# Edge passes of a graph network: gather in halves, bf16 scatter, packed control words, stored one-hots

## Time and profile before

| | |
|---|---|
| median of 3 runs | 13450.17 us (13437.72 to 13457.99) |
| span of the profiled execution | 13453.0 us |
| the three message layers | from about 1688 to 4347 us |
| relation pass | 4689 to 5909 us |
| two SAGE passes | 5946 to 7141 us |
| attention and the end | from about 7150 us |
| busy: TensorE, VectorE, ScalarE, GpSimd | 83%, 81%, 39%, 18% |

### The profile page before, as it was taken

One profiled execution on the slowest core, in us unless ns is written; L12 is line 12 of the kernel. 1 busy time (PEld: TensorE's weight loads), 2 busy tenths in 40 slices (PEclk: granted clock), 3 DMA queues, 4 the chain that ended last, 5 costly groups with the idle time before them and its releaser, 6 DMA issues. The chain is left out here.

```text
span 13453.0 us, 456368 instructions
## 1 busy us (share of the span) xinstructions
PE 11137.4 (83%) x106911; PEld 9882.7 (73%) x106912; DVE 10911.2 (81%) x40164; ACT 5227.5 (39%) x19100; POOL 2409.1 (18%) x7659
## 2 busy tenths in 40 slices
PE   3555399899899599976665879999998789999998
PEld 3444388799798499975553339999997338999998
DVE  6545399688688288876565999999997999999998
ACT  1000022122222022235452338865453337875454
POOL 2777300000000000001110001112221001222222
PEclk9999999899899599999896999999998999999999
DMA  1111177444243011113231554432221554432222
GB/s 54 47 50 47 45 228 236 138 128 128 80 128 115 4 41 41 41 50 88 71 87 51 148 140 115 115 92 73 70 73 47 143 147 113 115 98 73 70 73 61
DMA packets 1206840, 1232.94 MB, mean 92 GB/s; under 512 B 218352, under 2 KB 1042801, under 8 KB 1206107
## 3 DMA queue, kind: packets, MB, share of 16 engines
q1 hardware_dynamic: 1180954, 1228.47, 32.8%
q0 software_dynamic: 25792, 3.35, 0.2%
HBM read 1115.06 MB, written 116.16 MB: 92 GB/s over the span
## 5 line engine op out<-in xcount | busy, mean ns | idle before, releaser
L993 DVE TENSOR_SCALAR hot<-iota_row,place 128x128 f32<-128x128 f16 (+1 forms) x9000 | 1818.8, 269 | 158.5 <-PE acc L1092 135.7
L1711 ACT ACTIVATE msgs<-G,share 128x64 f32<-128x64 f32 x6000 | 1395.6, 315 | 1346.0 <-PE G L1725 1346.0
L985 DVE TENSOR_SCALAR hotT<-idx,iota_col 128x512 bf16<-128x512 f16 x4500 | 1323.8, 352 | 524.4 <-PE G L1138 492.1
L1725 PE MATMUL G<-u_b,hotT 128*128 x12000 | 1592.2, 276 | 50.3 <-DVE hotT L1659 50.3
L1735 PE MATMUL S<-msgs,hot 128*128 128x128 f32 x12000 | 1586.3, 275 | 0.0
L1157 ACT CAST msgs<-G 128x384 bf16<-128x384 f32 x2250 | 1020.4, 480 | 1372.7 <-PE G L1138 1368.1
L1725 PEld LDWEIGHTS G<-u_b,hotT 128*128 128x128 f32 x12000 | 1467.4, 193 | 51.0 <-issue 51.0
L1735 PEld LDWEIGHTS S<-msgs,hot 128*128 128x128 f32 x12000 | 1462.3, 192 | 0.0
L1080 PE MATMUL G<-table_m,hotT 128*128 x9000 | 1309.8, 248 | 93.4 <-issue 69.3
L1110 ACT ACTIVATE msgs<-sums 128x128 f32<-128x128 f32 x2250 | 699.3, 311 | 1762.3 <-DVE sums L1102 1400.5
L1547 ACT ACTIVATE msgs<-G,msgs 128x64 f32<-128x64 f32 x6000 | 1315.5, 333 | 30.5 <-issue 21.0
(11 more groups left out here) (323 smaller groups left out, 19877.9 us busy)
## 6 DMA issues: line engine op xcount, KB each, us to landing
idx<-pos_rows SPq DMA_DIRECT2D x6375, 128.0 KB, 2.9
hotT<-hots_d SPq DMA_DIRECT2D x750, 256.0 KB
hots_d<-hotT SPq DMA_DIRECT2D x375, 256.0 KB, 3.4
key_b<-key_rows SPq DMA_DIRECT2D x62, 416.0 KB
ty_b<-type_rows SPq DMA_DIRECT2D x62, 416.0 KB
rows<-rel_rows SPq DMA_DIRECT2D x1500, 6.0 KB
ew_now<-ew_rows_d SPq DMA_DIRECT2D x1125, 3.0 KB
sorted_d<-recs,place POOLq DMA_INDIRECT x806
```

Source lines behind the costliest of these rows:

```text
L985: op = eng.tensor_scalar(hotT[:, c % deep, n], idx[:, c, r], p.col[:, first:first + 1], None, ALU.is_equal)
L993: op = eng.tensor_scalar(hot[:, c % 2, q], p.row16[:], place[:, c % 2, q:q + 1], None, ALU.is_equal)
L1711: op = eng.activation(msgs[:, c % 2, 2 + j // HEADS, j % HEADS * D:(j % HEADS + 1) * D], G[c % 2][1][:, j * D:(j + 1) * D], ACT.Copy, scal ...
L1725: mm = eng.matmul(G[c % 2][b][:, k * W:(k + 1) * W], hotT[:, c % 2, q * P:(q + 1) * P], table[:, ds(dst_at(at, q, 24 * W), W)], start=True ...
```

## The change

1. **Control words.** The message, relation and SAGE passes use one packed word a group: four destination blocks of five bits each and the source block above them. TensorE reads eight turns' words, and three or two earlier ones for the scatter that lags, at once at the head of each loop body. The offset is worked out in registers: shift, remainder by 32, times 64. The tables for the attention passes stay.
2. **Gather in two halves (message pass).** The three bf16 parts of a table are now three planes. Per side a product of 128 columns (parts 0 and 1) and one of 64 (part 2) with the same weights; the second adds onto part 1's columns. The edge weight is one product of 64 columns, with nine rows that hold all pairs of parts. ScalarE copies the second half of the result out, VectorE adds the first.
3. **Scatter in three bf16 products (message pass).** ScalarE's relu writes fp32; its upper 16 bits, read as bf16 with a step of two, are part 0. VectorE subtracts them, then GpSimd again, for parts 1 and 2. Each chunk has three products of 64 columns, and in layer 0 one of two columns for the degrees. The scatter lags three turns.
4. **Stored one-hots.** Layer 0 makes the gather and the scatter one-hots (two of the four scatter ones on ScalarE, as relu(1 - |distance|)) and stores three kinds. Layers 1 and 2 read two kinds and make the destination one on VectorE. The relation pass reads the scatter kind, SAGE both the scatter and the source kind, and SAGE's second half of the eviction goes to VectorE. DMAs move two turns at once, through rings of eight turns.
5. The accumulator is laid out without gaps, 64 columns a block.

The core of the diff, with new functions:

```diff
+                four = blocks[0:1, dst, :].rearrange("o (t c) -> o t c", c=4)
+                lead = blocks[0:1, src, :].rearrange("o (t c) -> o t c", c=4)[:, :, 0:1]
+                one = p.ctl[0:1, 0:QUARTERS].unsqueeze(2)
+                chain(eng, v, [lambda: eng.tensor_copy(upper[0:1], four[:, :, 3:4])]
+                      + [lambda c=c: eng.scalar_tensor_tensor(upper[0:1], upper[0:1], 32.0, four[:, :, c:c + 1], ALU.mult, ALU.add)
+                         for c in (2, 1, 0)]
+                      + [lambda: eng.tensor_copy(one, upper[0:1]),
+                         lambda: eng.tensor_copy(upper_i[0:1], lead),
+                         lambda: eng.tensor_scalar(upper_i[0:1], upper_i[0:1], 20, None, ALU.logical_shift_left),
+                         lambda: eng.tensor_tensor(one, one, upper_i[0:1], ALU.bitwise_or)])
+                for table, plus, times in ((2, 2 * D, SMALL), (3, SMALL, SMALL)):
...
+def load_packed(p, eng, t, count):
+
+    of = p.ctl[0:1, ds(t, count)]
+    _, words = p.nc.values_load_multi_w_load_instructions(
+        of, [eng.engine], min_val=0, max_val=WORD,
+        skip_runtime_bounds_check_because="the table is computed here from block numbers that are clamped to 0..24")
+    return words
+
+
+def dst_block(word, q, times=D):
+
+    return (((word >> 5 * q) if q else word) % 32 * times).with_bounds(min_val=0, max_val=(BLK - 1) * times)
+
+
+def src_block(word, times=D):
+
+    return ((word >> 20) * times).with_bounds(min_val=0, max_val=(BLK - 1) * times)
...
+def tensor_turns(p, eng, step, lag):
+
+
+    words = load_packed(p, eng, 0, 8)
+    for t in range(8):
+        step(t, t, words[t], words[t - lag] if t >= lag else None)
+    with eng.Fori(1, QUARTERS // 8) as i:
+        words = load_packed(p, eng, i * 8 - lag, 8 + lag)
+        for c in range(8):
+            step(i * 8 + c, c, words[c + lag], words[c])
+    first, n = QUARTERS // 8 * 8, QUARTERS % 8
+    words = load_packed(p, eng, first - lag, n + lag)
+    for c in range(n + lag):
+        step(first + c, (first + c) % 8, words[c + lag] if c < n else None, words[c])
...
+def gnn_layer(p, s, l, degrees):
...
+    Q, LAG = QUARTERS, 3
+    make = l == 0
+    rows = [s.pos_rows[0], s.pos_rows[1]] if make else [s.pos_rows[1]]
+    NR = len(rows)
+    ND = NR + 1 + (0 if make else 1)
...
+                def lowest(t, c):
+                    ready(eng, lefted, t + 1)
+                    eng.tensor_tensor(msgs[:, c % 4, 2], msgs[:, c % 4, 1], upper[:, c % 4, 1], ALU.subtract
+                                      ).then_inc(made.h, 1)
...
+                def one_hots(t, c):
+                    if c % 2 == 0:
+                        ready(eng, idx_in[c // 2], first_uses(t, c, 16 * ND) + 16 * ND)
+                        if make:
+                            ready(eng, stored[c // 2], first_uses(t, c, 16))
+                    ready(eng, gathered, t - 7)
+                    for r in range(NR):
+                        op = eng.tensor_scalar(hots[:, c, KINDS - NR + r], idx[:, c, r], p.col[:, 0:1], None, ALU.is_equal)
+                    op.then_inc(turned.h, 1)
+
+                def add(t, c):
+                    ready(eng, halved, t + 1)
+                    ready(eng, relud, t + 1)
+                    eng.tensor_tensor(sums[:, c % 4], both(c)[:, :, 0], half[:, c % 4], ALU.add).then_inc(added.h, 1)
+
+                def remains(t, c):
+                    ready(eng, relud, t + 5)
+                    eng.tensor_tensor(msgs[:, c % 4, 1], msgs[:, c % 4, 0], upper[:, c % 4, 0], ALU.subtract
+                                      ).then_inc(lefted.h, 1)
+
+                def scatter_hots(t, c):
+                    ready(eng, placed, t + 1)
+                    for q in range(2):
+                        eng.tensor_scalar(hots[:, c, 0, q * P:(q + 1) * P], p.row16[:], place[:, c % 4, q:q + 1], None,
+                                          ALU.is_equal)
+
+                def step(t, c, pair):
+                    if not (isinstance(t, int) and t >= Q - 2):
+                        one_hots(t + 2, (c + 2) % 8)
+                    add(t, c)
+                    if make:
+                        scatter_hots(t, c)
+                    if not isinstance(t, int) or t > 0:
+                        remains(t - 1, (c - 1) % 8)
...
+                def relu(t, c):
+                    ready(eng, added, t + 1)
+                    ready(eng, scattered, t + 1)
+                    eng.activation(msgs[:, c % 4, 0], sums[:, c % 4], ACT.Relu).then_inc(relud.h, 1)
+
+                def step(t, c, pair):
+                    if make:
+                        distances(t, c)
+                    ready(eng, gathered, t + 1)
+                    ready(eng, added, t - 3)
+                    eng.copy(half[:, c % 4], both(c)[:, :, 1]).then_inc(halved.h, 1)
+                    if not isinstance(t, int) or t > 0:
+                        relu(t - 1, (c - 1) % 8)
+                    if make:
+                        scatter_hots(t, c)
...
+                def gather(t, c, at):
+                    ready(eng, turned, t + 1)
+                    ready(eng, added, t - 3)
+                    of = src_block(at)
+                    for q in range(4):
+                        to = G[c % 4][:, q * 2 * D:(q + 1) * 2 * D]
+                        for side in range(2):
+                            hot = hots[:, c, 1 + side, q * P:(q + 1) * P]
+                            table = s.table3[side][:, :, ds(dst_block(at, q) if side else of, D)]
+                            eng.matmul(to.rearrange("p (i f) -> p i f", f=D), hot, table[:, 0:2],
+                                       start=(side == 0), stop=False, skip_group_check=True)
+                            eng.matmul(to[:, D:2 * D], hot, table[:, 2], start=False, stop=False, skip_group_check=True)
+                        mm = eng.matmul(to[:, 0:D], s.ew_now[:, c, q * P:(q + 1) * P], s.we9[:, l], start=False, stop=True,
+                                        skip_group_check=True)
+                    mm.then_inc(gathered.h, 1)
+
+                def scatter(t, c, was):
+                    ready(eng, made, t + LAG + 1)
+                    for q in range(4):
+                        hot = hots[:, c, 0, q * P:(q + 1) * P]
+                        if degrees:
+                            eng.matmul(acc[:, BLK * D:BLK * (D + 2)][:, ds(dst_block(was, q, 2), 2)],
+                                       hot, p.onesb[:], start=False, stop=False, skip_group_check=True)
+                        to = acc[:, ds(dst_block(was, q), D)]
+                        for part in range(3):
+                            mm = eng.matmul(to, hot, upper[:, c % 4, part, q], start=False, stop=False, skip_group_check=True)
+                    mm.then_inc(scattered.h, 1)
+
+                def step(t, c, at, was):
+                    if at is not None:
+                        gather(t, c, at)
+                    if was is not None:
+                        scatter(t - LAG, (c - LAG) % 8, was)
...
+def parts_pass(p, s, row, tables):
...
+                def gather(t, c, h, at):
+                    of = src_block(at)
+                    for k in range(2):
+                        q = 2 * h + k
+                        for r in range(NT):
+                            mm = eng.matmul(G[c % 2 * 2 + h][:, k * 3 * D:(k + 1) * 3 * D].rearrange("p (q f) -> p q f", f=D),
+                                            hotT[:, c % DEEP, r, q * P:(q + 1) * P] if make else hot[:, c, 1, q * P:(q + 1) * P],
+                                            tables[r][:, :, ds(of, D)], start=(r == 0), stop=(r == NT - 1))
+                    mm.then_inc(gathered[h].h, 1)
+
+                def scatter(t, c, h, was):
+                    for k in range(2):
+                        q = 2 * h + k
+                        to = acc[:, ds(dst_block(was, q), D)]
+                        for part in range(3):
+                            mm = eng.matmul(to, hot[:, c, 0, q * P:(q + 1) * P],
+                                            msgs[:, c % 4, q, part], start=False, stop=False, skip_group_check=True)
+                    return mm
...
-        s.table3 = [p.sb("table_m0", [P, BLK * 3 * D], BF16, ctx), p.sb("table_m1", [P, 2 * FIVE * 512], BF16, ctx)]
+        s.table3 = [p.sb(f"table_m{i}", [P, 3, BLK * D], BF16, ctx) for i in range(2)]
...
-        s.hots_d = p.dram("hots_d", [QUARTERS, P, 2 * 4 * P], BF16)
-        s.ew_rows = p.dram("ew_rows_d", [EW, CHUNKS * P], BF16)
+        s.hots_d = p.dram("hots_d", [PAIRS, P, 2, KINDS * 4 * P], BF16)
+        s.ew_rows = p.dram("ew_rows_d", [EW_ROWS, CHUNKS * P], BF16)
```

More of the change, by code:

```diff
@@ new lines, in eights, with first_uses, ready, quarters_in @@
+def eights(eng, step):
+    for t in range(8):
+        step(t, t, t // 2)
+    with eng.Fori(1, QUARTERS // 8) as i:
+        for c in range(8):
+            step(i * 8 + c, c, i * 4 + c // 2)
+    for t in range(QUARTERS // 8 * 8, QUARTERS):
+        step(t, t % 8, t // 2)
```

(75 more changed lines are left out.)

389 lines of the change are left out of this document (162 added, 227 removed).

## The result

The changed kernel takes **15,048.6 us** (median of 4 runs, 15,045.1 to 15,059.1) against 13,452.1 (4 runs, 13,437.7 to 13,458.0): a ratio of 1.119, 95% interval 1.117 to 1.121. The forecast was 13,900, with a range of 13,200 to 14,450. Slower was right; the size was not, and the measured time lies above the range.

A forecast was written before the change was run, and what follows sets the result against it. TensorE's instruction queue was taken to bound layers 1, 2 and SAGE, VectorE layer 0, TensorE the relation pass. 366 + 302 - 85 - 138 + 5 = +450 on 13453.0, so 13,900 us; range 13,200 to 14,450.

The forecast's parts named there:

- The other engines ... All are covered: Layer 0: VectorE under 2.24, ScalarE under 2.4, GpSimd 0.57 us, all hidden under a turn of 3.04 us.
- Words: All six edited passes: one load per eight turns, 70 ns a word, 877 ns for eleven words, 110 a turn.
- Second address: Message gather on TensorE's queue: 32 + 77 = 109 ns each, five a turn (one source, four destinations).
- Unpacking, reuse: Message address arithmetic: gather destinations 103 + 3 x 142 ns, source 85; scatter reuses fields in five turns of eight, averaging 271.
- rival 1: Unpacking nearly free: shift and remainder add nothing to address instructions; -286 us, 13,167 us in all; chance 0.13.
- rival 3: A field needs two instructions in gather and scatter unpacking; 14,420 us in all; chance 0.12.
- rival 4: Nothing is reused in the scatter, as more values must be held for longer; +275 us, 14,175; chance 0.08.
- rival 2: Message gather's second address is folded into the instruction before, 0.545 us less a turn; 13,289 us in all; chance 0.12.
- what a queue that never pauses looks like: Layer 1 and SAGE before: nearly equal gaps of 77 and 72 ns per instruction, read as TensorE's queue never pausing.
- Relation -85: Relation pass: the queue stays ahead, TensorE's products remain, 3.0 us a turn; -0.226 x 375 = -85 us.
- SAGE -138: Two SAGE passes: queue of 7.6 instructions at 72 ns beyond 766 ns, 1.313 us a turn; -0.184 x 750 = -138 us.
- Products: Layers 1 and 2: TensorE's products fall to 1.14 us a turn, 2.3 at half clock, still covered by the queue's 2.57.

The follow-up runs named there:

- experiment 1: Changed kernel with its word load replaced by one load of twelve words from a multiple of four (14,529 us) or by two loads (14,596 us).
- experiment 2: Changed kernel with layer 0's store issued one step (two turns) later: 14,661 us; with the twelve-word load as well, 14,258 beside 13,508 for the kernel before.
- experiment 5: Kernel before, words loaded three turns at a time: 13,629 us beside 13,508; separately, kernel before with messages and scatter one-hots in BF16: 13,455 beside 13,508.
- experiment 3: Changed kernel without the third bf16 part in the gather (its 64-column product and second address): layers 1 and 2 at 2.328 and 2.331 us a turn.

## Why the forecast was wrong

Two steps failed. In the six edited passes the forecast was +445 us and the measurement +1,542. The two edits of experiments 1 and 2, made together, give back 851 of these 1,097: 531 by the load of words (1.42 us over the six turn lengths, by 374.5) and 319 by the place of the store (0.85). Neither step alone would have brought the time into the range: 15,049 less 531 is 14,518, less 319 it is 14,730.

**Layer 0, +302 forecast, +836 measured: a wait that was put at nothing.** The step "The other engines ... All are covered" priced each engine's work and took what is covered for free. It left out SyncE's queue. The store waits for GpSimd's last subtraction, and the loads for the next two turns stand behind it; the time of two turns is the sum of a circle over VectorE, GpSimd, SyncE and a landing. The error of 1.43 us a turn comes apart in what the experiments took out: 0.85 the store's wait, 0.22 the load, 0.26 the degrees beyond 0.47 (0.15 of it the slower load, last section), and 0.10 that is left, the price of the second addresses below. It could have been read from the kernel: SyncE's step of two turns ends with `store`, which waits for `made`, and the next step's loads come behind it.

**Words, 110 ns a turn forecast, 330 measured: the larger of the two errors.** The slope of 70 ns a word came from loads of four and eight words that start at a multiple of four words. It was carried to a load that neither starts so nor reads a multiple of four. (2,636 - 877) / 8 = 0.22 us a turn in layers 1 and 2, (2,402 - 877) / 8 = 0.19 in the others. Mending it measured 0.22 in layers 1 and 2, 0.30 in the relation pass and 0.23 in SAGE. The relation pass loses more than the load's own time. TensorE stood idle there for 0.26 us a turn with the load of ten words and for 0.06 with that of twelve; its granted clock was 0.96 in the one stretch and 1.00 in the other, which would be some 0.1 us of a turn by an estimate from these two. The two parts were not separated by a run.

**Second address: 109 ns forecast, 128 measured by the same reckoning.** Its record is 51 ns and not 32: +0.10 us a turn. With both corrections the new turn is 2.57 + 0.22 + 0.10 = 2.89 us, and it measures 2.905 and 2.901. Instructions (16.4 a turn by 16.9 forecast) and the gap (80 ns by 77) were nearly right. The Trainium skill ("Perfetto Trace Analysis", Sequencer-only Instruction) has the fetch, the wait and the semaphore push of such an instruction outside its record. The trace agrees, with 80 ns an instruction in this queue; which of the three fills them it does not show.

**Unpacking, reuse: right.** The five first addresses of the gather record 607 ns a turn by 614 forecast (85 + 529); a scatter field 71 by 68. Rivals 1, 3 and 4 are out by the rows themselves, rival 2 by experiment 3.

**What bounds before: half right.** Naming the queue in layers 1, 2 and SAGE led to nearly the right cost of the new turn, since in the changed kernel the queue is by far the longest. But in experiment 5 a lighter queue did not make before faster. The step "what a queue that never pauses looks like" was an inference from an even gap, and it does not hold: waits for VectorE hide in it.

**Relation -85 and SAGE -138: near but for the load.** With twelve-word loads they measured (3.104 - 3.240) x 374.5 = -51 and, twice, (1.312 - 1.495 + 1.294 - 1.497) x 374.5 = -145. The relation pass keeps 0.10 us a turn more than the 3.00 forecast; why was not tested. SAGE's sum came out in part by luck: it had 7.6 queue instructions with a gap of 72 ns, and the kernel with both edits has 6.6 with 80 to 83.

**Products: covered, as forecast,** in spite of the clock. Layer 1's granted clock was 0.85 and layer 0's 0.51, and the turn lengths of layer 1 came out of the queue alone.

## What to carry to other kernels

Before counting a new wait as covered, read the queue that it stands in to the end: the transfers behind a store in one engine's queue belong to the time of its wait, and moving a store by one step, or to a queue with room, can be cheap to try (it gave 0.85 us and 0.64 us a turn here). A price measured on a few cases of an instruction holds for cases like them in size and in place, and the next case should be priced from both ends. And a change that packs several ideas should be taken apart: the losing and the gaining half of this one, separated, gave 1.1%, once a queue that the mixture had filled was relieved.

## What the runs showed that was not expected

A load of registers from the control table has two prices. From a multiple of four words, 4, 8 and 12 words take 336, 590 to 600 and 850 ns. From other starts, 9, 10 and 11 words take 2,170, 2,402 and 2,636 ns, 240 a word. The Trainium skill ("Runtime: NRT & Kernel Launch", Instruction fetch mechanics) gives some 200 ns a register, in bulk too; its page speaks of loads from HBM, and the table here lies in SBUF. The slow loads are near that figure; the fast ones, at 71 to 84 ns a word, are not, and there the measurement decides. Whether the start, the number of words or the registers they are loaded into makes the difference was not separated.

In layer 0 with the degrees, once the store no longer held the pass, the same load took 1.2 us longer than in layer 1: 2,078 ns in place of 850 with twelve words, 3,853 in place of 2,637 with eleven. It follows the loop's branch back, and the body of eight turns has some 740 instructions of TensorE where it has some 640 without the degrees. The Trainium skill says in the same section that after a taken branch to a block that is no longer at hand execution waits until it is fetched. No run here shows whether that is the cause, and with the store in its old place the time did not appear.

The gap beyond the record of an instruction of TensorE's queue was 79 to 80 ns in layer 0 and layer 1 of three kernels (the changed one's layer 1, both passes with both edits, layer 0 without the degrees), with 64 to 72 weight loads and products a turn between them.
